# A vision tower on one core: the attention probabilities are turned by true transposes and normalised in place, where products with a diagonal of reciprocals did both

## What is computed

```python
q, k, v = jnp.split(x @ w_attn + b_attn, 3, axis=-1)      # heads of 16 channels
scores = jnp.einsum('bhid,bhjd->bhij', q * scale, k)
scores = scores + jnp.einsum('bhid,jd->bhij', q * scale, rel)
scores = jnp.where(causal, scores, -jnp.inf)              # 196 x 196
probs = jax.nn.softmax(scores, axis=-1)
y = jnp.einsum('bhij,bhjd->bhid', probs, v)
```

## Time and profile before

| | before |
|---|---|
| median of 3 runs | 7268.11 us (7267.75 to 7270.31) |
| profiled execution, first to last instruction (span) | 7259.2 us |
| median less span | 8.9 us |
| TensorE busy | 6605.1 us (91%) |
| VectorE busy | 5383.8 us (74%) |
| ScalarE busy | 3644.6 us (50%) |
| GpSimd busy | 3111.4 us (43%) |
| mean granted TensorE clock | 0.906 |
| L714, TensorE, matmul records | 9216, 1175.1 us |
| L502, GpSimd | 512, 608.4 us |

### The profile page before, as it was taken

One profiled execution on the slowest core, in us unless ns is written; L12 is line 12 of the kernel. 1 busy time (PEld: TensorE's weight loads), 2 busy tenths in 40 slices (PEclk: granted clock), 3 DMA queues, 4 the chain that ended last, 5 costly groups with the idle time before them and its releaser, 6 DMA issues.

```text
span 7259.2 us, 167273 instructions
## 1 busy us (share of the span) xinstructions
PE 6605.1 (91%) x56000; PEld 5936.7 (82%) x56000; DVE 5383.8 (74%) x15934; ACT 3644.6 (50%) x12160; POOL 3111.4 (43%) x4048
## 2 busy tenths in 40 slices
PE   4999999999999999999999999999999999999998
PEld 4888888888888888888888888888888888888887
DVE  3777777777777777777777777777777777777776
ACT  1545555554555455545545554555455455545554
POOL 4444444444444444444444444444444444444443
PEclk8889899999899998989989998999899999899998
DMA  4211121112111111211121111112111211121110
GB/s 46 29 22 23 22 29 22 23 22 29 22 23 26 25 23 22 27 23 23 22 29 22 23 25 25 23 22 28 23 23 22 29 22 23 22 29 22 23 24 8
DMA packets 228657, 175.83 MB, mean 24 GB/s; under 512 B 27785, under 2 KB 228126, under 8 KB 228630
## 3 DMA queue, kind: packets, MB, share of 16 engines
q1 hardware_dynamic: 218934, 173.46, 18.4%
q10 hardware_dynamic: 8336, 1.07, 0.2%
q0 software_dynamic: 1360, 0.96, 0.1%
HBM read 156.11 MB, written 19.27 MB: 24 GB/s over the span
## 4 chain that ended last, share of the span: by engine, by line
issue 34%; PE 20%; DVE 18%; POOL 15%; POOLq 9%; DVEq 3%; ACT 1%; ACTq 0%
PE bank L693 7%; POOL diag L502 6%; DVE qz L1109 5%; POOL rstd L487 4%; PE bank L645 4%; DVE negmax L1128 2%; DVE z L1062 2%; PE bank L681 2%; POOLq L556 2%; POOL h L557 2%; PE bank L781 2%; POOLq L486 2%; POOL res L565 2%; PE bank L792 2%; POOLq L582 2%
## 5 line engine op out<-in xcount | busy, mean ns | idle before, releaser
L1514 ACT ACTIVATE p<-bank,negmax 98x98 f32<-98x98 f32 (+1 forms) x3072 | 1132.3, 376 | 317.6 <-DVE negmax L1128 274.6
L714 PEld LDWEIGHTS bank<-diag,p 128*98 128x98 f32 x9216 | 1066.0, 202 | 157.1 <-issue 104.0
L714 PE MATMUL bank<-diag,p 128*98 128x98 f32 x9216 | 1175.1, 291 | 14.7 <-POOL diag L502 1.7
L1522 ACT COPY pT<-bank 98x392 f32<-98x392 f32 x768 | 374.7, 488 | 1542.2 <-PE bank L714 1542.1
L693 PE MATMUL bank<-tokw,x_sb 128*98 128x193 f32 x4096 | 924.3, 382 | 9.1 <-DVEq L1049 9.1
L502 POOL TENSOR_TENSOR diag<-ident,rden 98x588 f32<-98x588 f32 x512 | 608.4, 1199 | 648.2 <-DVE rden L1142 648.2
L693 PEld LDWEIGHTS bank<-tokw,x_sb 128*98 128x98 f32 x4096 | 825.0, 260 | 67.5 <-issue 29.2
L1128 DVE TENSOR_REDUCE negmax<-bank 98x1 f32<-98x196 f32 (+2 forms) x1536 | 626.1, 456 | 269.0 <-PE bank L681 268.7
L681 PE MATMUL bank<-qk_parts,qz 128*98 128x196 f32 (+1 forms) x6144 | 744.7, 265 | 0.0
L681 PEld LDWEIGHTS bank<-qk_parts,qz 128*98 128x98 f32 x6144 | 656.8, 166 | 11.4
L520 POOL TENSOR_TENSOR qz<-qk_parts,ones 32x588 fp32r<-32x588 f32 x256 | 301.2, 1176 | 721.8 <-DVE qk_parts L1099 701.5
(11 more groups left out here) (272 smaller groups left out, 14889.4 us busy)
## 6 DMA issues: line engine op xcount, KB each, us to landing
x_sb<-in_x SPq DMA_DIRECT2D x384, 196.0 KB, 4.8
x_sb<-in_x SPq DMA_DIRECT2D x384, 189.0 KB, 8.0
out<-out_row SPq DMA_DIRECT2D x128, 147.0 KB
x_store<-in_L_tok_W SPq DMA_DIRECT2D x6, 96.0 KB
diag<-in_L_ffn_W SPq DMA_DIRECT2D x1, 576.0 KB
gstore<-in_L_ffn_W SPq DMA_DIRECT2D x1, 384.0 KB
p<-in_L_attn_w_attn ACTq DMA_DIRECT2D x2, 96.0 KB
gstore<-in_L_ffn_W ACTq DMA_DIRECT2D x1, 192.0 KB
```

The source lines that it names most:

```text
L714: last = mm(bank[b][0:HT, HT * i:HT * i + HT], src, diag[:, h // 3, t, h % 3], start=True, stop=True)
L1514: sc.activation((p1 if t else p0)[0:HT, 3 * s + g], bank[b][0:HT, c0:c0 + (T if t else HT)], ACT.Exp, bias=negmax[:, s, t, g:g + 1], accum ...
L1522: sc.copy(pt_dst(name[0], int(name[1:])), bank[RING[name]][0:HT, 0:4 * HT]).then_inc(sem["pT_act"], 1)
```

## The change

The diagonals go. GpSimd multiplies the exponentials of a set by the reciprocals where they lie, in `p0` and `p1`: two instructions for each set (98 x 294 and 98 x 588) in place of one (98 x 588). TensorE then makes true transposes of the blocks with the identity, of 98 partitions, where it made products over 128 partitions with the diagonals. The semaphore is renamed, its counts stay. The place of the raw weights gets a tensor of its own, `stage`, which isn't cleared.

```diff
@@ semaphores
-    ... h1b_sb=1, diag_sb=4, ...
+    ... h1b_sb=1, pnorm_sb=4, ...
@@ tensors
-        diag = sb("diag", [128, 4, 2, NG, HT])
+        stage = sb("stage", [128, F // 128 * D + 2 * D])
@@ GpSimd, before the loop
-            for t in (p1, diag):
-                gp.memset(t[:], 0.0)
+            gp.memset(p1[:], 0.0)
@@ GpSimd, in step
-                def diagonals(s):
+                def normalised(s):

                     gp.wait_ge(sem["rden_sb"], after("rden_sb", n, s + 1))
-                    gp.tensor_tensor(
-                        diag[0:HT, s].rearrange("p t g i -> p (t g) i"),
-                        ident[0:HT, 0:HT].unsqueeze(1).broadcast_to([HT, 2 * NG, HT]),
-                        rden[:, s].rearrange("p t g -> p (t g)").unsqueeze(2).broadcast_to(
-                            [HT, 2 * NG, HT]), ALU.mult).then_inc(sem["diag_sb"], 1)
+                    for t, part, w in ((0, p0, HT), (1, p1, T)):
+                        heads = part[0:HT, NG * s:NG * s + NG]
+                        last = gp.tensor_tensor(
+                            heads, heads, rden[:, s, t].unsqueeze(2).broadcast_to([HT, NG, w]),
+                            ALU.mult)
+                    last.then_inc(sem["pnorm_sb"], 1)
...
-                    diagonals(0)
+                    normalised(0)
...
@@ TensorE, transposes
-                        src = p1[:, h, HT * u:HT * u + HT] if t else p0[:, h]
-                        last = mm(bank[b][0:HT, HT * i:HT * i + HT], src, diag[:, h // 3, t, h % 3],
-                                  start=True, stop=True)
+                        src = p1[0:HT, h, HT * u:HT * u + HT] if t else p0[0:HT, h]
+                        last = pe.transpose(bank[b][0:HT, HT * i:HT * i + HT], src,
+                                            ident[0:HT, 0:HT])
                     last.then_inc(sem["p_T"], 1)
@@ TensorE, causal
-                        pe.wait_ge(sem["diag_sb"], after("diag_sb", n, s + 1))
+                        pe.wait_ge(sem["pnorm_sb"], after("pnorm_sb", n, s + 1))
```

More of the change, by code:

```diff
@@ L80 @@
     nT_sb=1, expz=1, kk_sb=1, vv_sb=1, nsel_sb=1, qs_sb=1, probs2=1, p2T_sb=1, z3T_sb=1, gelu_sb=3,
-    qz2_sb=2, f1b_sb=1, sqsum_sb=1, tok_rstd=1, y_rstd=1, h1_sb=1, h1b_sb=1, diag_sb=4, h1_rstd=1, h2_rstd=1, res_sb=1, h3_rstd=1,
+    qz2_sb=2, f1b_sb=1, sqsum_sb=1, tok_rstd=1, y_rstd=1, h1_sb=1, h1b_sb=1, pnorm_sb=4, h1_rstd=1, h2_rstd=1, res_sb=1, h3_rstd=1,
 )
@@ L276, in build @@
             raw[name] = flat[:, i * size:(i + 1) * size].rearrange("p (c w) -> p c w", c=2)
-        flat = diag[:].rearrange("p s t g i -> p (s t g i)")
+        flat = stage
         size = F // 128 * D
@@ L542, in step @@
                 if front:
-                    diagonals(1)
+                    normalised(1)
                 if head:
@@ L550, in step @@
                 if front:
-                    diagonals(2)
-                    diagonals(3)
+                    normalised(2)
+                    normalised(3)
                 if head:
```

## The result

| | before | changed |
|---|---|---|
| time, median of four runs | 7269.04 us (7267.75 to 7270.31) | 7141.43 us (7138.35 to 7144.61) |
| ratio, with its 95% interval | 1 | 0.9823 [0.9809, 0.9837] |
| span of the profiled execution, mean granted clock | 7259.2 us, 0.906 | 7136.6 us, 0.872 |

The change makes the kernel 1.8% faster: 127.6 us where 223 were forecast. The direction was right and the time lies in the range, but the gain is a little over half of what was forecast.

A forecast was written before the change was run, and what follows sets the result against it. TensorE, busy 91% of the span, came first, with VectorE ending waits inside each image. A gain of 1.73 us for each of 128 images plus 2 us at the start, 223 us, took 7268 to 7045 us; range 6950 to 7230.

The forecast's parts named there:

- Half the passes: TensorE's L714: one pass a block for two, 36 fewer an image, 3.4 us at full clock, 6.4 us at the lower.
- (a): Wait before L627: GpSimd's set takes 1.86 us, L1071 waits for 0.66 us of it, `mTs` comes 0.55 us earlier.
- (b), (c): Quick image, L627 to `z3`: L844 ends at 2922.6 for 2924.21, then VectorE from `merge` limits; 1.2 us gained.
- GpSimd dearer: Rival: 2.3 us a set, `mTs` gains only 0.1 us, `y_row` and `ctxT` end 0.4 us later; 7155 us, chance 0.07.
- (d): Slow image, bound by TensorE: L858 starts 4.1 us earlier, 1.6 us lost behind it to the lower clock; 2.5 us gained.
- (e): Before L801: `qb` (L1256) meets GpSimd's longer L541 in some images, so TensorE waits; costs 0.12 us an image.
- The sum: Whole kernel, half quick and half slow images: 1.85 less 0.12 is 1.73 us an image, 223 us in all, 7045 us.
- The clock: L627 to `z3`, lower clock until the values' products are done: quick image gains nothing, slow 4.1 us, mean 2.0 us.
- Lower clock through the projection: Rival: lower clock in every image through the projection, 55.4 us an image, 7230 us; chance 0.17.
- Back only in the MLP: Rival: full clock returns only in the MLP, the clock staying low beside transposes; chance 0.07.
- The change doesn't do it: Rival, L714: a transpose of fp32 data still takes two passes; 7268 us, chance 0.02.
- Better: Rival: quick images gain 1.2 us and slow ones recover as early, average gain some 3.2 us; 6860 us, chance 0.07.

The follow-up runs named there:

- filled kernel: Changed kernel plus 20 products that nobody reads, in TensorE's wait before L627: 6713.78 us, ratio 0.92.
- filled kernels: Unread products in the wait before L627: 18 in the kernel before (6778.63 us, ratio 0.9288), 20 in the changed kernel (6713.78 us, ratio 0.92).

## Why the prediction was right in direction and its gain too high by 95 us

*Half the passes.* Right: 4608 records, at 0.177 us for a block at the lower clock. The filled kernel shows the price at full clock: 12 blocks in 1.22 us, 4 in 0.54, so (1.22 - 0.54) / 8 = 0.085 us for a block more, where 0.094 was taken. A block went from two passes to one, as the rows had it.

*(a) The wait itself.* Right: `mTs` was to come 0.55 us earlier, and A0 to L627 is 0.49 us shorter. GpSimd's set has 1.90 us for 1.86, and L1071 0.82 for 0.8. The waits before A2 and L627 are 2.84 us together; 2.5 to 3.3 was forecast for L810, L818 and L627. That 0.80 us of it would fall to A2, behind `y_row`, was not seen and costs nothing.

*(b), (c) The quick image gains 1.2 us.* Half right. The limit was named rightly: with the clock kept up it is VectorE, and TensorE waits before `z3` (1.65 us in the filled kernel, 1.3 forecast). But in the changed kernel no image of the 121 keeps its clock there, so none takes this path. And the 1.2 us count on TensorE's `scatter` as what holds `merge` up before. In the quick image it did, with 3.4 us of the lower clock behind L627. With the clock up it doesn't, even before the change: from A0 to `z3` the filled kernels differ by 0.27 us, which is 0.43 from the earlier `mTs` less 0.16 in the stretch (9.46 for 9.30 us), where `y_row` ends behind GpSimd's second pair. The walk left `y_row` out; the prediction has it only under "GpSimd dearer".

*(d) The slow image gains 2.5 us.* It gained more, 58.64 - 54.61 = 4.0 us for the 22 images of its kind. The paragraph on the clock had this case, with 4.1 us, and its stretch of 15.00 - 3.5 = 11.5 us was measured at 11.52.

*(e) 0.12 us for `qb`.* It is nothing. In the changed kernel L1256 takes 427 ns at most, so `qb` meets L541 in no image, and TensorE waits for `qb` 2.5 us in the whole run, as before:

```profile
L1256 DVE TENSOR_TENSOR qb<-qs,slot_of x128: 414/416/427, 178.2 to 7099.8; 128x256 f32<-128x256 f32 x128
```

What is longer ahead of A0 goes with the lower clock there, 3.4 us for 2.4.

*The sum, the step that failed.* Of the two ways of the prediction the one under "The clock" is what happened: every image at the lower clock until the values' products are done (0.50 until 11.2 us behind the start of L627 in the median image). There it said that the mean was 2.0 us, about the same as in the sum, and that the forecast held for both. That the sum of (c) and (d) came out near this is luck: no image took their path. The 2.0 us failed at two terms.

The first is the weights, "half quick, half slow". They came from the span's mean clock between two images. Counted, 65 of 122 were quick, 33 slow and 24 in between, so that the mean stretch was 12.43 us and not 12.9. Against that 11.52 and 0.49 leave 12.43 - 11.52 + 0.49 = 1.40 us an image, not 2.0.

The second is the embedding. The prediction let it run on as before. The changed kernel has the lower clock there in every image, the kernel before had it in 85 of 122: 0.48 us an image. 1.40 - 0.48 = 0.92 us, which is the 0.93 measured. For a quick image with no lower clock in the embedding (52.76 us, 13 of them) the change costs 1.85 us, for the common quick one (54.30 us, 52 of them) 0.3 us, and the forecast had 0.15 us.

*The rivals.* Lower clock through the projection: no, `z3` to L635 takes 1.94 us as before, at a granted clock of 1.00 (3040.90 to 3042.85). Back only in the MLP: no, by the same window. GpSimd dearer: no, 1.90 us a set. The change doesn't do it: no, 4608 records. Better: the quick image's clock was recovered in none. The mean image lies in the forecast's 53.3 to 54.7 us, which is too wide to tell the two ways apart.

**What stays open** is why the clock falls where it does. It falls 0.9 us behind the start of L627 in 115 of the changed kernel's 121 images, and 0.4 to 0.8 us behind in the others. With products in place of transposes it falls mostly 0.5 to 0.6 us behind, and the stretch is 3.47 us longer, 20 passes' worth. In the kernel before it varied from image to image, from 0.25 us ahead of that start to 1.1 us behind it, in an order that repeats. In the changed kernel the same length came image after image, and moving set 3 alone didn't disturb it. Six products at a busy place changed more than their own length. No run tells what sets this pattern, and without it the time of an unfilled variant can be forecast only to within the lengths seen, 54.6 to 58.0 us.

## What to carry to other kernels

Before costing an edit that makes TensorE wait longer, look at the granted clock behind the wait. Standing still for 2 us once an image cost more here (3.35 us of 54.6) than the whole change gave (0.93), and twenty products whose result nobody reads, placed exactly in the wait, gave it back (51.26 us an image). What the halved passes were worth hung on the clock too: 3.39 us an image at the lower one, 0.14 us with the clock kept up. Count the kinds of images over the whole trace before weighting them, and give every stretch of the image its own clock, not only the one that the edit touches. Look at the clock behind every wait that an edit makes: here the filled wait before L627 didn't cover the one of 1.14 us before A4, behind which the image had 5.7 us at 0.50.

## What was not expected of the hardware

In the changed kernel and in the one with products for transposes, waits of 1.3 to 2.0 us before L627 were followed by a granted clock of 0.50 over 10.2 and 13.6 us of each image, and it went when the wait of the changed kernel was filled (mean clock 0.990 for 0.872). With twenty transposes of 98 x 98 in the wait the mean clock was 0.991, with twenty products 0.990. Six products out of twenty, with 1.27 us of the wait left, brought the time at 0.50 from 13.6 to 6.2 us an image.

VectorE's two-operand instructions at L1071 and L1072 took 0.36 us each beside an idle GpSimd, and 0.82 and 1.23 us beside its products, ending some 0.2 us behind one of them. The cost of GpSimd's work, measured in the filled kernel, was this and the longer `y_row`, 1.74 us an image, and not the transposes' own waiting: L714 of the changed kernel waited for it 4.5 us in the whole run.
